# A three-layer EdgeConv plus relational graph network on one core: rows that no edge owns are skipped by the gathers instead of fetched

## The chip, the cores and the metric

The kernel runs on one core of a Trainium2 chip. The metric is the device time of one execution in microseconds (us). The core has five engines that matter here: TensorE (PE in the profile, PEld for its weight loads), VectorE (DVE), ScalarE (ACT), GpSimd (POOL) and SyncE (SP, which issues most DMAs). An indirect DMA, which fetches one table row for each of up to 128 partitions by a list of row numbers, is issued by POOL.

## The reference, cut to what matters

There are 12,500 nodes with 128 features and 212,500 directed edges sorted by destination. Three layers of edge convolution are followed by one relational layer:

```python
def _edge_conv(x, src, dst, W1, b1, W2, b2, n_nodes):     # three times, relu between
    xi = x[dst]
    xj = x[src]
    m = jnp.concatenate([xi, xj - xi], axis=-1)
    h = jax.nn.relu(m @ W1 + b1) @ W2 + b2
    agg = jax.ops.segment_max(h, dst, num_segments=n_nodes)
    return jnp.where(jnp.isfinite(agg), agg, 0.0)
...
x = _layernorm(x + edge_conv_stack(x))
# relational layer: row = src + n * rel, inv = 1 / count of row
msg = x[dst] * inv[row][:, None]
agg = segment_sum(msg, row).reshape(r, n, e)
x = _layernorm(x + relu(einsum('rij,rnj->ni', weights, agg)))
```

## The kernel before

**Tiles of edges.** `m @ W1` is split into a part that depends on the destination node (a table in SBUF, `table`) and a part that depends on the source node (a table in device memory, `tab_b`, 12,544 rows of 128 floats). Edges are cut into tiles of 128, and a tile holds edges of one super block of 256 destination nodes only. Each of the 49 super blocks begins a new tile, so the last tile of a super block is filled up with positions whose edges belong to the next super block. There are `NT` = 1,712 tiles of 128 positions, 219,136 positions for 212,500 edges, so 6,636 positions are owned by no edge (3.03%). From the inputs, the super blocks need 1,684 tiles, with 3,052 unowned positions in them, and the 28 last tiles (3,584 positions) are unowned altogether. The fourth gather stage (below) cuts the same number of edges, sorted by source, into `NT2` = 1,708 tiles, with 6,124 unowned positions (2.80%).

**What an unowned position does before the change.** In the first three stages it keeps the source number of the edge that stands there (or a number from the padding), and its row is fetched and computed. Its place in the block, `loc_f`, is `OUT_OF_BLOCK` (256), so the one-hot matrices ignore it. In the fourth stage its row number is its position in the tile (0 to 127), from `iota`.

**A layer's loop.** Tiles are taken in groups of `GT` = 4. For each group POOL issues four indirect DMAs (`gather_body`, L857), each fetching 128 rows of `tab_b` (128 floats each) into one of `HG` = 4 buffers `rows`. POOL waits with `s_p1` until PE has used the buffer four groups ago, and every four groups for the list of row numbers (`s_idx`, copied by ACT, L1323). PE transposes the gathered rows into PSUM (L977), adds the destination part by one-hot products (L979), multiplies by `W2` (L986), and transposes back after the maximum scan (L1001). ACT evicts (L1341, L1353) and copies the block's table rows (L1332). DVE makes the one-hot matrices (L1637, L1639) and does the scan (L1666). SP stores the scanned rows and loads the block numbers. 428 groups make a layer, 1,712 gathers. Between layers POOL fetches the last row of each node (`gather_ends`, L840, 98 indirect DMAs, three times in all).

**The relational stage.** With z = x times each relation's weights stored as `z_tab` (100,352 rows), POOL fetches four tiles per group again (`gather_products`, L918, 427 groups, 1,708 gathers, buffers `got`). PE multiplies each by a one-hot matrix (L1225), which ACT makes (L1416, L1425), and DVE adds the product to the accumulator (L2146).

**Where the row numbers are made.** `edge_stage` (DVE, seven times, each with two sets of 128 tiles) reads windows of destinations and sources, in four parts; PE turns `src_f` and DVE copies it to `idx_all`. `window_work` (DVE, seven times) does the same for the relational stage, with `row2`, and `any2` for the unowned positions. `key_windows` (L865) is one indirect DMA with only 50 partitions (`NST` = 50), and L823 is another; both fetch 512 bytes for each partition.

The order on each engine is the order in which the program is written. Semaphores alone connect the engines.

Of the kernel before, what the change touches and what calls it, by code (L numbers as in the profile page):

```python
# [25 lines left out]
I32 = mybir.dt.int32  # L26
# [6 lines left out]
P = 128  # L33
EPS = 1e-5
BIG = 3.3895313892515355e38
OUT_OF_BLOCK = 256
GT = 4
HG = 4
# [7 lines left out]
def gnn_kernel(nc, x, src, dst, etype, params, w_rel, out):  # L46
    N, C = x.shape
    E = dst.shape[0]
    R = w_rel.shape[0]
    assert C == P  # L50
    NB = -(-N // P)
# [27 lines left out]
    OUT2 = 2 * W2P - 1  # L79
# [22 lines left out]
    with ExitStack() as ctx:  # L102
# [3 lines left out]
        def sem(name):  # L106
            return ctx.enter_context(nc.semaphore(name))
# [7 lines left out]
        iota = sb("iota", [P, P])  # L115
# [35 lines left out]
        a = Area(agg, NBT * P)  # L151
# [29 lines left out]
        a = Area(work, WORK)  # L181
# [14 lines left out]
        a = Area(agg, NBT * P)  # L196
        idx = [a.cut(HT, I32) for _ in range(2)]
# [4 lines left out]
        rows = [a.cut(GT * P).rearrange("p (t f) -> p t f", f=P) for _ in range(HG)]  # L202
# [12 lines left out]
        a = Area(tab_a, TAB)  # L215
# [7 lines left out]
        src_f = [a.cut(P) for _ in range(2)]  # L223
        loc_f = [a.cut(P) for _ in range(2)]
        starts = [a.cut(P) for _ in range(2)]
        stops = [a.cut(P) for _ in range(2)]

        a = Area(work, WORK)
# [95 lines left out]
        def meta_of(k, f, t):  # L325
            at = (k % LG * 4 + f) * GT + t
            return meta[k // LG][:, at:at + 1]
# [42 lines left out]
        s_rows = [sem(f"s_rows{k}") for k in range(HG)]  # L370
        s_st = [sem(f"s_st{k}") for k in range(2)]
        s_sent = sem("s_sent")
        s_found = sem("s_found")
        s_ecol = sem("s_ecol")
        s_base = sem("s_base")
# [431 lines left out]
        def _(pool):  # L807
# [35 lines left out]
            for l in range(3):  # L843
                if l > 0:
                    for c in range(NC):
                        gather_ends(l, c, c % 2)
                for s in range(2):
                    pool.wait_ge(s_bd[s], 8 * NC * (l + 1))
                def gather_body(i, many=LG):
                    for k in range(many):  # L850
                        at = Lt(l, i, k)
                        if at.j == 0:
                            pool.wait_ge(s_idx[at.h], at.n + 1)
                        pool.wait_ge(s_p1, at.G + 1)
                        tick()
                        for t in range(GT):
                            g.indirect_dma_start(rows[at.j][:, t, :], None, tab_b,  # L857
                                                 bass.IndirectOffsetOnAxis(
                                                     ap=idx[at.h][:, at.j * GT + t:at.j * GT + t + 1], axis=0)
                                                 ).then_inc(s_rows[at.j], 16)  # L860

                def key_windows():
                    pool.wait_ge(s_rk, RK_WIN)
                    tick()
                    g.indirect_dma_start(win2_i, None, key_s.rearrange("(a n) -> a n", a=1),  # L865
                                         bass.IndirectOffsetOnAxis(ap=at2, axis=1)).then_inc(s_kwin, 16)

                def pair_windows(n):
                    pool.wait_ge(s_pairs, 16)
                    pool.wait_ge(s_from2, n + 1)  # L870
                    tick()
                    for s in range(2):
                        g.indirect_dma_start(win2[s].rearrange("p e f -> p (e f)"), None,
                                             pairs.rearrange("n f -> (n f)").rearrange("(a n) -> a n", a=1),
                                             bass.IndirectOffsetOnAxis(ap=from2[s], axis=1)).then_inc(s_win2[s], 16)

                if l < 2:
                    with loop(pool, 0, NL) as i:
                        gather_body(i)
                else:  # L880
                    with loop(pool, 0, 9) as i:
                        gather_body(i)
                    key_windows()
                    with loop(pool, 9, WIN_BODY) as i:
                        gather_body(i)
                    for n in range(NQ // 2):
                        pair_windows(n)
                        with loop(pool, WIN_BODY + 2 * n, WIN_BODY + 2 * n + 2) as i:
                            gather_body(i)
                    with loop(pool, WIN_BODY + NQ, NL) as i:  # L890
                        gather_body(i)
                gather_body(NL, many=OV)
                if l == 0:
                    pool.wait_ge(s_af, NC + 1)
                    g.iota(row_base, [[GT * P, NTP // GT], [1, GT]], base=1 - GT, channel_multiplier=0, **exact
                           ).then_inc(s_base, 1)
                if l == 1:
                    pool.wait_ge(s_keys, 16)
                if l == 2:
                    for s in range(2):  # L900
                        pool.wait_ge(s_crs[s], 16 * (NQ // 2))
                for s in range(2):
                    pool.wait_ge(s_st[s], 16 * (NG // 2) * (l + 1))
                pool.wait_ge(s_sent, 16 * (l + 1))
                if l == 0:
                    pool.wait_ge(s_er, 6)
# [4 lines left out]
            def gather_products(i, many):  # L911
                for k in range(many):
                    if k % LG == 0:
                        pool.wait_ge(s_cr[k // LG], 16 * (i + 1))
                    pool.wait_ge(s_pr, i * LR + k + 1)
                    tick()
                    for t in range(GT):
                        g.indirect_dma_start(got[k % HG][:, t, :], None, z_tab,  # L918
                                             bass.IndirectOffsetOnAxis(ap=meta_of(k, 0, t).bitcast(I32), axis=0)
                                             ).then_inc(s_got[k % HG], 16)  # L920

            with loop(pool, 0, NL2) as i:
# [545 lines left out]
        def _(dve):  # L1468
# [87 lines left out]
            def edge_stage(n, part):  # L1556

                if part == 0:
                    dve.wait_ge(s_win[min(n, 1)], 64 if n == 0 else 32 * (NQ - 2))
                    for s in range(2):  # L1560
                        v.tensor_copy(win_base[s], base_f[:, 2 * n + s:2 * n + s + 1])
                        v.tensor_copy(dst_f[s], dst_w[2 * n + s])
                        last = v.tensor_copy(src_f[s], src_w[2 * n + s])
                    last.then_inc(s_wv, 1)
                elif part == 1:
                    dve.wait_ge(s_wv, n * WV + 1)
                    for s in range(2):
                        v.tensor_scalar(loc_f[s], dst_f[s][:, 1:P + 1], win_base[s], float(OUT_OF_BLOCK), ALU.subtract, ALU.min)
                        v.tensor_tensor(starts[s], dst_f[s][:, 1:P + 1], dst_f[s][:, 0:P], ALU.not_equal)
                        last = v.tensor_tensor(stops[s], dst_f[s][:, 1:P + 1], dst_f[s][:, 2:P + 2], ALU.not_equal)  # L1570
                    last.then_inc(s_wv, 1)
                elif part == 2:
                    dve.wait_ge(s_wv, n * WV + 2)
                    for s in range(2):
                        v.tensor_scalar(starts[s], starts[s], -2.0, 1.0, ALU.mult, ALU.add)
                        last = v.tensor_scalar(stops[s], stops[s], -float(OUT_OF_BLOCK), float(OUT_OF_BLOCK), ALU.mult, ALU.add)
                    last.then_inc(s_wv, 1)
                else:
                    dve.wait_ge(s_wv, n * WV + 3)
                    for s in range(2):  # L1580
                        after(dve, s_store[s], 48 * n)
                    for s in range(2):
                        v.tensor_scalar(cut_b[s], starts[s], BIG, None, ALU.mult)
                        v.tensor_copy(loc_b[s], loc_f[s])
                        last = v.tensor_tensor(stops[s], stops[s], loc_f[s], ALU.max)
                    last.then_inc(s_wv, 1)

# [337 lines left out]
            def window_work(n, part):  # L1925
# [23 lines left out]
                elif part == 5:  # L1949
                    dve.wait_ge(s_wv2, 4 * n + 2)  # L1950
                    for s in range(2):
                        v.scalar_tensor_tensor(out=row2[s], in0=loc2[s], scalar=float(OUT2), in1=row2[s],
                                               op0=ALU.is_lt, op1=ALU.mult)
                        last = v.scalar_tensor_tensor(out=any2[s], in0=loc2[s], scalar=float(OUT2), in1=iota[:, :],
                                                      op0=ALU.is_ge, op1=ALU.mult)
                    last.then_inc(s_wv2, 1)
                elif part == 6:
                    dve.wait_ge(s_wv2, 4 * n + 3)
# [252 lines left out]
```

## Time and profile before

| | |
|---|---|
| median of 3 runs | 9462.51 us (9452.86 to 9466.43) |
| profiled execution, its own time | 9459.5 us |
| its span, first to last instruction | 9457.6 us |
| POOL busy | 6941.5 us (73%) |
| PE busy | 6691.3 us (71%) |
| DVE, ACT busy | 56%, 52% |
| mean granted TensorE clock | 0.91 |

The page gives busy time of each engine, groups of instructions by source line with the idle time ahead of them and what ended it, and the timeline gives single instructions. Idle time marked "issue" is time in which the engine waited for nothing that the profile shows. Register and semaphore instructions are not counted as busy.

### The profile page before, as it was taken

What the parts mean: (1) busy time and instruction counts of PE and PEld (TensorE: products, weight loads), DVE (VectorE), ACT (ScalarE), POOL (GpSimd) and SP (SyncE); (2) the same over time, 40 slices, a digit from 0 to 9 for tenths busy, and PEclk for the clock granted to TensorE, in tenths of its full rate; (3) what the DMA queues carried; (4) which work ended last, traced back from release to release, by engine and by line L of the source; (5) the groups of instructions that cost most, each with busy time, mean ns of one, the idle gap of its engine ahead of it and who ended that gap; (6) DMA issues with size and microseconds to landing.
All of it is one profiled execution on the core that took longest, in us unless ns stands there. A gap on an engine that the chain in (4) does not pass through costs nothing.

```text
span 9457.6 us, 159685 instructions
## 1 busy us (share of the span) xinstructions
PE 6691.3 (71%) x41098; PEld 5236.2 (55%) x41098; DVE 5269.7 (56%) x9597; ACT 4895.9 (52%) x11866; POOL 6941.5 (73%) x7196
## 2 busy tenths in 40 slices
PE   6777777876677777777667777777768555555555
PEld 6666666665555666666555665666644333333333
DVE  4666667665577666667546555555556333333334
ACT  3444444443344444444434444444446777777776
POOL 5777777776777777777777777777764777777775
PEclk9999999998899999989989999999999777777777
DMA  6665666664455555565545666656656222222222
GB/s 161 159 160 158 159 158 160 156 161 120 134 153 148 151 152 151 148 148 147 148 127 152 165 160 163 162 156 159 157 158 240 54 54 54 54 54 54 54 54 67
DMA packets 896218, 1260.59 MB, mean 133 GB/s; under 512 B 185847, under 2 KB 601079, under 8 KB 895270
## 3 DMA queue, kind: packets, MB, share of 16 engines
q1 hardware_dynamic: 650494, 784.23, 27.5%
q0 software_dynamic: 230048, 471.99, 22.9%
q8 instruction: 158, 2.59, 0.1%
q10 hardware_dynamic: 15408, 0.88, 0.1%
q14 instruction: 110, 0.90, 0.0%
HBM read 834.14 MB, written 424.01 MB: 133 GB/s over the span
## 4 chain that ended last, share of the span: by engine, by line
POOL 17%; issue 12%; PE 11%; DMA 7%; DVE 2%; ACT 1%; POOLq 0%; DVEq 0%; ACTq 0%; SPq 0%
POOL agg L857 10%; PE ps L1225 6%; POOL work L918 6%; DMA work<-z_tab,work 4%; DMA agg<-tab_b,agg 3%; PE ps L979 2%; POOL work L840 1%; DVE tab_a L2146 1%; PE ps L1201 1%; PE ps L1202 1%; PE ps L977 1%; ACT agg L1274 0%; PE ps L986 0%; ACT tab_a L1425 0%; DVE work L2168 0%
## 5 line engine op out<-in xcount | busy, mean ns | idle before, releaser
L857 POOL DMA_INDIRECT agg<-tab_b,agg x5136 | 4991.5, 972 | 1625.4 <-issue 1533.1
L979 PE MATMUL ps<-tab_a 128*128 128x128 f32 x20544 | 3076.1, 284 | 1.9 <-issue 1.9
L979 PEld LDWEIGHTS ps<-tab_a 128*128 128x128 f32 x20544 | 2872.3, 202 | 2.4 <-issue 2.4
L977 PE MATMUL ps<-ident,agg 128*128 128x128 f32 x5136 | 1480.4, 288 | 1600.8 <-DMA agg<-tab_b,agg 1517.3
L1666 DVE TENSOR_TENSOR_SCAN agg<-agg,ps 128x512 f32<-128x512 bf16 x1284 | 1639.5, 1277 | 1693.6 <-PE ps L986 1691.3
L1341 ACT ACTIVATE agg<-ps 128x512 f32<-128x512 f32 x1284 | 766.5, 597 | 3483.6 <-PE ps L979 3459.4
L918 POOL DMA_INDIRECT work<-z_tab,work x1708 | 1611.8, 944 | 576.2 <-issue 454.4
L1225 PE MATMUL ps<-tab_a,work 128*128 128x256 f32 x3416 | 1224.3, 521 | 917.9 <-DMA work<-z_tab,work 634.4
L977 PEld LDWEIGHTS ps<-ident,agg 128*128 128x128 f32 x5136 | 752.7, 147 | 1836.7 <-issue 1409.3
L1332 ACT ACTIVATE tab_a<-tab_a 128x256 f32 x5136 | 1714.1, 404 | 59.0 <-issue 48.2
L1225 PEld LDWEIGHTS ps<-tab_a,work 128*128 128x128 f32 x3416 | 839.4, 257 | 1303.2 <-DVE tab_a L2146 1110.6
L2146 DVE TENSOR_TENSOR tab_a<-ps,tab_a 128x256 f32 x1708 | 724.3, 424 | 1417.2 <-PE ps L1225 1246.2
L986 PE MATMUL ps<-agg,w 128*128 128x512 f32 x2568 | 1342.5, 605 | 0.0
L1425 ACT ACTIVATE tab_a<-tab_a,work 128x256 f32<-128x256 f32 x1708 | 883.7, 588 | 469.0 <-issue 469.0
L1637 DVE SCALAR_TENSOR_TENSOR tab_a<-agg,pidx,ps 128x512 f32<-128x512 bf16 x1284 | 933.1, 727 | 45.6 <-ACT agg L1341 44.1
L1639 DVE SCALAR_TENSOR_TENSOR tab_a<-agg,pidx_up,ps 128x512 f32<-128x512 bf16 x1284 | 950.1, 740 | 0.0
L1001 PEld LDWEIGHTS ps<-ident,agg 128*128 128x128 f32 x5136 | 610.0, 141 | 469.1 <-issue 464.3
L1001 PE MATMUL ps<-ident,agg 128*128 128x128 f32 x5136 | 787.3, 276 | 4.7 <-DVE agg L1666 2.3
L1416 ACT ACTIVATE tab_a<-work 128x256 f32<-128x256 f32 x1708 | 727.4, 496 | 59.7 <-DMA work<-col_rel 5.1
L1353 ACT ACTIVATE agg<-ps 128x512 f32<-128x512 f32 x1284 | 738.3, 575 | 17.6 <-PE ps L1001 14.5
L1658 DVE TENSOR_SCALAR agg<-iota_b,agg 128x128 bf16<-128x128 bf16 x1712 | 331.4, 275 | 457.8 <-PE ps L993 440.8
L840 POOL DMA_INDIRECT work<-scan_rows,endrow x294 | 288.7, 982 | 194.3 <-issue 99.6
(252 smaller groups left out, 2963.3 us busy)
## 6 DMA issues: line engine op xcount, KB each, us to landing
agg<-row_two SPq DMA_DIRECT2D x1284, 256.0 KB
scan_rows<-agg SPq DMA_DIRECT2D x1284, 256.0 KB
agg<-tab_b,agg POOLq DMA_INDIRECT x5136
z_tab<-tab_a SPq DMA_DIRECT2D x84, 512.0 KB, 3.7
work<-z_tab,work POOLq DMA_INDIRECT x1708
tab_b<-work SPq DMA_DIRECT2D x42, 448.0 KB, 3.1
work<-in_x SPq DMA_DIRECT2D x26, 448.0 KB, 5.3
z_tab<-work SPq DMA_DIRECT2D x14, 512.0 KB, 3.8
```

Source lines behind the costliest of these rows:

```text
L857: g.indirect_dma_start(rows[at.j][:, t, :], None, tab_b, bass.IndirectOffsetOnAxis(ap=idx[at.h][:, at.j * GT + t:at.j * GT + t + 1], axis= ...
L918: g.indirect_dma_start(got[k % HG][:, t, :], None, z_tab, bass.IndirectOffsetOnAxis(ap=meta_of(k, 0, t).bitcast(I32), axis=0)).then_inc(s_ ...
L977: mm(to, rows[at.j][:, t, :], ident[:, :], is_transpose=True, start=True, stop=False)
L979: last = mm(to, tabs[at.s][:, t, h * P:(h + 1) * P], hot_t[at.s][:, h, t * P:(t + 1) * P], start=False, stop=(h == 1))
L986: mm(ps[:, 2 + at.s, :], w2[:, l], h1[at.s], start=True, stop=True).then_inc(s_p2, 1)
L1001: last = tr(ps[:, 4 + at.s, t * P:(t + 1) * P], scan[at.s][:, t * P:(t + 1) * P], ident[:, :])
L1225: last = mm(flat[:, to:to + W2P], got[k % HG][:, t, :], hot_r[k % 4][:, t, :], start=True, stop=True)
L1332: last = a_(tabs[s][:, t, :], table[:, bass.ds(blk[t] * W2P, W2P)], ACT.Copy)
L1425: last = a_(hot_r[k % 4][:, t, :], off_r[k % 2][:, t, :], ACT.Relu, scale=meta_of(k, 3, t), bias=meta_of(k, 2, t))
L1637: v.scalar_tensor_tensor(out=hot_t[at.s][:, 0, :], in0=locs[at.k], scalar=pidx[:, 0:1], in1=ps[:, at.s, :], op0=ALU.is_equal, op1=ALU.bypass)
L1639: v.scalar_tensor_tensor(out=hot_t[at.s][:, 1, :], in0=locs[at.k], scalar=pidx_up[:, 0:1], in1=ps[:, at.s, :], op0=ALU.is_equal, op1=ALU.b ...
L1666: v.tensor_tensor_scan(scan[at.s], cuts[at.k], ps[:, 2 + at.s, :], scan[1 - at.s][:, GT * P - 1:GT * P], ALU.min, ALU.max).then_inc(s_scan, 1)
```

## The change

Four things are edited. (1) In `edge_stage` the source number of an unowned position becomes `NB * P` = 12,544, one beyond the last row of `tab_b`: a new tile `off_f` is made by one tensor_scalar for each set and merged by one maximum. (2) In `window_work` an unowned position gets row number `NB * P * R` = 100,352, one beyond `z_tab`, in place of its position in the tile. (3) All gathers of `gather_body` and `gather_products` get a highest allowed number (`bounds_check`) and `oob_is_err=False`, by which a number beyond it makes no transfer and no error. The bound is handed to the instruction in a register, and the built program sets that register ahead of each of these gathers. The other indirect DMAs are as before. (4) Since a skipped row keeps what its buffer held, POOL clears the four buffers `rows` (128 x 512 floats each) once ahead of the first layer's gathers, and waits for it.

```diff
+        off_f = [a.cut(P) for _ in range(2)]
...
+        s_clean = sem("s_clean")
...
                 for s in range(2):
                     pool.wait_ge(s_bd[s], 8 * NC * (l + 1))
+                if l == 0:
+                    for k in range(HG):
+                        g.memset(rows[k], 0.0).then_inc(s_clean, 1)
+                    pool.wait_ge(s_clean, HG)
...
                             g.indirect_dma_start(rows[at.j][:, t, :], None, tab_b,
                                                  bass.IndirectOffsetOnAxis(
-                                                     ap=idx[at.h][:, at.j * GT + t:at.j * GT + t + 1], axis=0)
+                                                     ap=idx[at.h][:, at.j * GT + t:at.j * GT + t + 1], axis=0),
+                                                 bounds_check=NB * P - 1, oob_is_err=False
                                                  ).then_inc(s_rows[at.j], 16)
...
                         g.indirect_dma_start(got[k % HG][:, t, :], None, z_tab,
-                                             bass.IndirectOffsetOnAxis(ap=meta_of(k, 0, t).bitcast(I32), axis=0)
+                                             bass.IndirectOffsetOnAxis(ap=meta_of(k, 0, t).bitcast(I32), axis=0),
+                                             bounds_check=NB * P * R - 1, oob_is_err=False
                                              ).then_inc(s_got[k % HG], 16)
...
                         v.tensor_scalar(starts[s], starts[s], -2.0, 1.0, ALU.mult, ALU.add)
+                        v.tensor_scalar(off_f[s], loc_f[s], float(OUT_OF_BLOCK), float(NB * P), ALU.is_ge, ALU.mult)
...
                         v.tensor_copy(loc_b[s], loc_f[s])
+                        v.tensor_tensor(src_f[s], src_f[s], off_f[s], ALU.max)
...
-                        last = v.scalar_tensor_tensor(out=any2[s], in0=loc2[s], scalar=float(OUT2), in1=iota[:, :],
-                                                      op0=ALU.is_ge, op1=ALU.mult)
+                        last = v.tensor_scalar(any2[s], loc2[s], float(OUT2), float(NB * P * R), ALU.is_ge, ALU.mult)
```

Apart from the register, nothing else moves on any engine. On POOL, ahead of the first layer's loop, the program before has the last of the 28 window loads and then the jump into the loop (`tab_b` is the source table, `agg` the memory in which the buffers `rows` lie):

```order
L830 DMA work<-src_pad,tab_a 128x128
L878 UNCONDITIONAL_BRANCH
L878 BRANCH_PREFETCH_HINT
L878 ISA
L854 ISA
L857 DMA agg<-tab_b,agg 128x128 x4
```

In the changed program the same place reads:

```order
L832 DMA work<-src_pad,tab_a 128x128
L853 MEMSET agg 128x512 x4
L885 UNCONDITIONAL_BRANCH
L885 BRANCH_PREFETCH_HINT
L885 ISA
L860 ISA
L863 DMA agg<-tab_b,agg 128x128 x4
```

The four memsets stand ahead of the first gather, and the gathers themselves keep their number and order.

## Rows read from the trace of the kernel before

**Rows 1.** The page's part 1, busy us (share of span) xinstructions:

```profile
PE 6691.3 (71%) x41098; PEld 5236.2 (55%) x41098; DVE 5269.7 (56%) x9597; ACT 4895.9 (52%) x11866; POOL 6941.5 (73%) x7196
```

**Rows 2.** Groups of POOL: out<-in xcount | busy, mean ns | idle before:

```profile
L857 POOL DMA_INDIRECT agg<-tab_b,agg x5136 | 4991.5, 972 | 1625.4 <-issue 1533.1 <-PE ps L979 75.6 <-ACT agg L1323 16.5
L918 POOL DMA_INDIRECT work<-z_tab,work x1708 | 1611.8, 944 | 576.2 <-issue 454.4 <-PE ps L1225 65.8 <-DMA work<-col_rel 56.0
```

**Rows 3.** Timeline of POOL, first layer: start us, us, instruction, idle before:

```profile
1513.87 0.94 POOL L857 DMA_INDIRECT agg<-tab_b,agg  x1 [0.30 <-issue]
1515.12 0.94 POOL L857 DMA_INDIRECT agg<-tab_b,agg  x1 [0.30 <-issue]
1516.37 0.94 POOL L857 DMA_INDIRECT agg<-tab_b,agg  x1 [0.30 <-issue]
1517.61 0.94 POOL L857 DMA_INDIRECT agg<-tab_b,agg  x1 [0.30 <-ACT agg L1323]
...
1521.39 0.94 POOL L857 DMA_INDIRECT agg<-tab_b,agg  x1 [0.30 <-PE ps L979]
```

**Rows 4.** Each gather line by itself: duration ns min/median/max, first and last start:

```profile
L857 POOL DMA_INDIRECT agg<-tab_b,agg x5136: 938/944/4941, 108.8 to 7017.3; - x198
L918 POOL DMA_INDIRECT work<-z_tab,work x1708: 940/944/962, 7260.2 to 9391.3; - x190
```

**Rows 5.** Busy time by stretch: first layer, third layer, relational stage:

```profile
core 0: us, PE busy (x) PEld busy (x) DVE busy (x) ACT busy (x) POOL busy (x), PEclk, DMA share, GB/s
108.70:2248.00 2139.30, 1683.47 (x12790) 1358.23 (x12790) 1468.32 (x3675) 1013.81 (x2660) 1618.31 (x1710) 0.97 0.61 158
4841.00:7018.30 2177.30, 1642.67 (x11217) 1335.79 (x11218) 1187.53 (x1551) 1015.91 (x2660) 1650.24 (x1724) 0.97 0.61 158
7260.00:9393.00 2133.00, 1222.32 (x3408) 837.96 (x3408) 721.46 (x1702) 1594.50 (x3415) 1611.80 (x1708) 0.77 0.21 54
```

**Rows 6.** Groups of PE that wait for gathered rows:

```profile
L977 PE MATMUL ps<-ident,agg 128*128 128x128 f32 x5136 | 1480.4, 288 | 1600.8 <-DMA agg<-tab_b,agg 1517.3
L1225 PE MATMUL ps<-tab_a,work 128*128 128x256 f32 x3416 | 1224.3, 521 | 917.9 <-DMA work<-z_tab,work 634.4
```

**Rows 7.** POOL instructions with one call or other shapes, same columns as Rows 2:

```profile
L865 POOL DMA_INDIRECT work<-key_s,work x1 | 1.0, 957 | 0.3 <-issue 0.3
L823 POOL DMA_INDIRECT agg<-dst_pad,agg x1 | 1.1, 1106 | 15.6 <-DVE agg L1505 15.6
L810 POOL MEMSET agg<- 1x620 int32 x1 | 0.6, 604 | 0.3 <-POOLq L2199 0.3
```

**Rows 8.** Timeline ahead of the first gather, ACT and POOL:

```profile
102.73 0.21 ACT L1323 ACTIVATE agg<-idx_all 128x16 int32<-128x16 int32 x1 [0.25 <-issue]
108.77 0.94 POOL L857 DMA_INDIRECT agg<-tab_b,agg  x1 [27.14 <-issue]
```

**Rows 9.** DVE groups with the shapes of the added and replaced operations:

```profile
L1576 DVE TENSOR_SCALAR tab_a<-tab_a 128x128 f32<-128x128 f32 x14 | 3.4, 243 | 0.0
L1585 DVE TENSOR_TENSOR tab_a<-tab_a 128x128 f32<-128x128 f32 x14 | 4.0, 283 | 0.7 <-issue 0.7
L1954 DVE SCALAR_TENSOR_TENSOR work<-work,iota 128x128 f32<-128x128 f32 x14 | 4.0, 287 | 0.0
```

**Rows 10.** Timeline of POOL, second layer: gathers that took longer:

```profile
4399.81 3.09 POOL L857 DMA_INDIRECT agg<-tab_b,agg  x1 [0.31 <-issue]
4403.21 0.94 POOL L857 DMA_INDIRECT agg<-tab_b,agg  x1 [0.30 <-issue]
```

**Rows 11.** The page's part 3, queue: packets, MB, share of 16 engines:

```profile
q1 hardware_dynamic: 650494, 784.23, 27.5%
q0 software_dynamic: 230048, 471.99, 22.9%
```

## The prediction

> **What bounds the kernel now.** I read the busy shares first. No engine is full over the whole span: POOL has 73%, PE 71% [rows 1]. Such a share is an average over stages and hides what POOL's idle time is, so I went to the groups of POOL. The 5,136 gathers of the three layers and the 1,708 of the relational stage have 972 and 944 ns of busy time each, and almost all of the idle time before them is "issue", not a wait for anybody [rows 2]. The timeline shows the form of it: a gather of 0.94 us, 0.30 us of nothing, the next gather, without end, so one starts every 1.25 us [rows 3]. The reader should see that the gap is the same 0.30 us where the row names PE or ACT as the releaser. These are the group changes, at which POOL has a semaphore wait and a register operation of its own to do. So the released wait had long been satisfied, and the small sequencer work between two gathers costs nothing visible.
>
> Then the stretches: 1,712 gathers at 1.249 us are 2138 us, and the first layer's stretch is 2139 us. 1,708 at 1.249 are 2133 us, and the relational stage is 2133 us; the third layer's 2177 us hold some longer gathers [rows 5]. In these stretches POOL is the bound from the first gather to the last. In one group's 5.0 us PE works 1683/428 = 3.9 us in the layers (2.9 us in the relational stage, where ACT has 1594/427 = 3.7 us), and PE's largest wait is for the gathered rows [rows 5, 6]. The DMA engines are at 0.61 and 0.21 of their time, so transfers aren't what holds the queue up [rows 5]. The time of this kernel is therefore 6,844 times what POOL spends on one gather, plus stages that the change doesn't touch: each nanosecond on each gather is 6.84 us of the total, 0.07%. Everything below turns on what POOL pays for one gather with the bound and the skipping.
>
> **What the change removes.** It removes transfers: 3 x 6,636 + 6,124 = 26,032 rows of 512 bytes, 13.3 MB of the 472 MB that POOL's queue moves [rows 11]. I cost this at nothing, because what PE waits for is the gather that POOL hasn't issued yet, and not a long transfer. The cover is POOL's own pace: as long as gathers start 1.25 us apart and the DMA engines are 0.61 busy, a transfer that is 3% smaller only lands a little earlier in a wait that POOL ends. Nor does POOL issue fewer instructions: all 6,844 gathers stay, those of the 28 wholly unowned tiles too.
>
> Does a gather with fewer rows cost POOL less? The gathers of the relational stage lie between 940 and 962 ns over 1,708 of them [rows 4]. The one warm indirect DMA with 50 partitions in place of 128 (same 512 bytes each) took 957 ns, against 944; another with 50, the very first of the program, took 1106 [rows 7]. So 78 rows less bring nothing, and the 3.8 rows less in a mean gather should bring nothing either. For the other side, were the whole 944 ns proportional to rows, 3.03% would be 29 ns on each of 5,136 gathers and 2.80% 26 ns on 1,708: 147 + 45 = 192 us saved. That is the lower bound.
>
> **What the change adds to a gather.** First, a register set ahead of each. POOL's register operations at group changes lie inside the same 0.30 us gap [rows 3], so I take nothing; if it were exposed, it would lengthen the gap in each row. Second, the comparison of 128 numbers with the bound and the leaving out of rows on both sides, reads and writes. No row of the trace has such a gather. Its lower end is nothing, if the comparison fits beside work that takes 944 ns anyhow. For its upper end I take the nearest elementary work of POOL, one element after another in one partition: the memset of 620 elements took 604 ns, 0.97 ns each [rows 7], so 128 elements are 125 ns, or 6,844 x 0.125 = 855 us. Between the two I choose by the row that stands nearest, the warm 50-row gather: work per row is so small a part of a gather that 78 rows moved it by 13 ns at the most. I take 13 ns as the size of something small and real that is done for each gather, 6,844 x 0.013 = 89 us. That it is above zero is a judgement: instructions have to be executed for the check on the engine that has no slack, and 2.4 ns a gather are enough to be seen.
>
> The Trainium skill has a rule that speaks against the change more strongly. 
>
> **What it adds elsewhere.** The four memsets have 512 elements in each partition. At 0.97 ns these are 0.5 us each, 2.0 us, and about 0.3 us for the wait on `s_clean`. Queued behind them on POOL is the first gather, and everything waits for POOL from there on. The row numbers are ready at 102.9 us, and the first gather starts at 108.8 us, with nothing to wait for that is shown [rows 8], so POOL has a start-up of its own there that the memsets may partly overlap. I take 2.3 us in full. DVE gets 14 tensor_scalar of 243 ns and 14 maxima of 283 ns, 7.4 us in seven portions, and in the third layer 14 operations become 44 ns cheaper [rows 9]. DVE has 1468 us of work in a first layer of 2139 us [rows 5], and the six portions inside the layer end long before their row numbers are used. The first portion, 1.05 us, lies ahead of the last of the table stores that open the layer. Cost nothing; without that cover 1 us.
>
> **The sum.** Profiled time 9459.5 + 2.3 + 89 = 9551 us. The median of the runs is 3 us above this execution, so I say 9553 us, 1.0% slower.
>
> **The rivals.**
>
> A. *The check is free.* It hides beside the fixed part of a gather. For it: the constancy of 944 ns in all gathers whatever their data, and the hidden register work. Against it: POOL has no other work to hide it behind. Result 9462.5 + 2.3 = 9465 us. It holds while the extra is under (19 - 2.3)/6.84 = 2.4 ns.
>
> B. *A gather's cost falls with its rows.* This is the case on the other side. Place: the 0.94 us in each gather. Price: up to 192 us, so 9273 us; it decides as soon as a skipped row saves more than the check costs. For it: nothing but that rows must be written by somebody; against it the 50-row gather. A part of it, 20 to 60 us, is as likely as the whole.
>
> C. *The check works through the rows one by one with a decision on each.* Then a gather grows by more than the 125 ns of the upper end, and the kernel goes above 10,320 us. For example, if the 944 ns are 7.4 ns for each of 128 rows and a decision adds half of that, a gather grows by 472 ns and the kernel to 9462 + 3230 = 12,690 us; PE, ACT and DVE would only wait longer. Against it: 128 rows and 50 cost the same, so work seems not to go row by row. The skill's rule above would be this case.
>
> D. *Contention.* Single gathers of the second layer took 3.09 us [rows 10] beside DVE's sorting, which is why the mean of the layers is 972. If the new gather touches SBUF more, these grow. The whole excess before is 5,136 x 28 ns = 144 us, and doubling it gives +144 us: inside my case.
>
> **How the numbers follow.** A measurement of this kernel can tell about 0.2%, 19 us. My case, something small from 2.4 to 125 ns a gather: 0.42 (9482 to 10,320 us). A: 0.32. B: 0.18, of which 0.10 below 9400 us. C: 0.08. The range leaves out C and the far part of B, 0.18 in all, and so goes from 9400 to 10,320 us. My case alone, at 5 to 60 ns, would be 9500 to 9875 us. Faster 0.18, same 0.32, slower 0.42 + 0.08 = 0.50.
>
> **What would show it.** The profile after should have the gathers of both lines as before in number, with a median above 944 ns by 5 to 60 ns in the relational stage, where nothing disturbs them, or a gap longer than 0.30 us if the register work is exposed. The gathers of the 28 unowned tiles, the last ones of each layer, are the test of B: if they are shorter than the others, rows do cost. Packets of POOL's queue should fall by about 26,000. PE's wait for gathered rows should grow by what the gathers grow. I am wrong if the median stays at 944 (then A), if it falls, or if the added time sits at the start of the first layer instead of in every gather.

## The result

The changed kernel takes 9839.35 us (median of 4 runs, 9832.66 to 9853.8) against 9464.28 us (4 runs, 9452.86 to 9466.43). The ratio is 1.0402, with a 95% interval from 1.0389 to 1.0415. The direction was forecast; the size was not: 375 us instead of 91, or 4.0% instead of 1.0%.

The page of the changed kernel, in the form of [rows 1] (busy us, share of the span, instructions) and, for POOL's queue, of [rows 11] (packets, MB, share of the 16 engines):

```profile
PE 6833.1 (69%) x41098; PEld 5364.7 (54%) x41098; DVE 5276.5 (54%) x9625; ACT 4901.0 (50%) x11866; POOL 7331.0 (74%) x7200
...
q0 software_dynamic: 230048, 460.27, 20.9%
```

POOL has 389.5 us more to do with four instructions more. The groups of POOL (count, busy, mean ns of one, idle before) say where, and answer to [rows 2]:

```profile
L863 POOL DMA_INDIRECT agg<-tab_b,agg x5136 | 5286.3, 1029 | 1608.6 <-issue 1507.3 <-PE ps L987 98.0 <-ACT agg L1331 3.4
L925 POOL DMA_INDIRECT work<-z_tab,work x1708 | 1705.2, 998 | 576.1 <-issue 479.6 <-DMA work<-col_rel 56.0 <-PE ps L1233 40.5
...
L853 POOL MEMSET agg<- 128x512 f32 x4 | 1.9, 532 | 19.2 <-DMA tab_b<-work 19.2
```

The layers' gathers grew by 294.8 us and the relational stage's by 93.4 us, together 388.2 of the 394.3 us by which this execution (9853.8 us) is longer than the one profiled before (9459.5 us). The idle time between them didn't grow. Each line by itself (min/median/max ns, first and last start) shows that the gathers are longer throughout, the shortest too; compare [rows 4]:

```profile
L863 POOLq MOVE  x5136: 29/29/38, 105.2 to 7303.1; - x198
L863 POOL DMA_INDIRECT agg<-tab_b,agg x5136: 992/1000/5169, 112.2 to 7317.6; - x198
```

```profile
L925 POOL DMA_INDIRECT work<-z_tab,work x1708: 992/1000/1015, 7562.6 to 9787.0; - x190
```

The median rose from 944 to 1000 ns. 6,844 x 56 ns are 383 us, 2% above the measured 375. Below, the same form of gather has a median of 997 ns in four kernels, two of which are the changed one with a single edit, so 3 of the 56 ns belong to this execution or its chip. The MOVE that sets the bound's register takes 29 ns. The timeline of POOL in the first layer (start, us, instruction, idle before) shows the same 0.30 us gap as in [rows 3], so the MOVE lies inside it:

```profile
1513.91 1.00 POOL L863 DMA_INDIRECT agg<-tab_b,agg  x1 [0.30 <-issue]
1515.21 1.00 POOL L863 DMA_INDIRECT agg<-tab_b,agg  x1 [0.30 <-PE ps L987]
1516.52 1.00 POOL L863 DMA_INDIRECT agg<-tab_b,agg  x1 [0.30 <-issue]
```

What waits on POOL pays: PE's wait for the layers' rows rose from 1517.3 [rows 6] to 1687.0 us, and in the relational stage from 634.4 to 769.0 us.

### The profile page after: what moved, and what is told of

Its sections match the earlier page's. It is cut to its first block, busy times and chain, and to the rows that moved or that the text cites. A ratio compares the mean times of both kernels' runs of the same rounds, so it can differ in the third digit from the quotient of the medians.

```text
span 9851.9 us, 166561 instructions
## 1 busy us (share of the span) xinstructions
PE 6833.1 (69%) x41098; PEld 5364.7 (54%) x41098; DVE 5276.5 (54%) x9625; ACT 4901.0 (50%) x11866; POOL 7331.0 (74%) x7200
## 3 DMA queue, kind: packets, MB, share of 16 engines
q0 software_dynamic: 230048, 460.27, 20.9%
## 4 chain that ended last, share of the span: by engine, by line
issue 18%; POOL 15%; PE 9%; DMA 6%; DVE 1%; POOLq 1%; ACT 1%; ACTq 0%; DVEq 0%; SPq 0%
POOL agg L863 7%; POOL work L925 7%; PE ps L1233 4%; DMA agg<-tab_b,agg 3%; DMA work<-z_tab,work 3%; PE ps L987 2%; POOL work L842 1%; PE ps L985 1%; PE ps L1209 1%; PE ps L1210 1%; PE ps L994 0%; ACT agg L1282 0%; POOLq L925 0%; POOLq L863 0%; DVE work L2177 0%
## 5 line engine op out<-in xcount | busy, mean ns | idle before, releaser
L863 POOL DMA_INDIRECT agg<-tab_b,agg x5136 | 5286.3, 1029 | 1608.6 <-issue 1507.3
L987 PE MATMUL ps<-tab_a 128*128 128x128 f32 x20544 | 3163.8, 289 | 5.9 <-issue 5.9
L987 PEld LDWEIGHTS ps<-tab_a 128*128 128x128 f32 x20544 | 2949.7, 207 | 6.6 <-issue 6.6
L985 PE MATMUL ps<-ident,agg 128*128 128x128 f32 x5136 | 1503.7, 293 | 1789.7 <-DMA agg<-tab_b,agg 1687.0
L925 POOL DMA_INDIRECT work<-z_tab,work x1708 | 1705.2, 998 | 576.1 <-issue 479.6
L1233 PE MATMUL ps<-tab_a,work 128*128 128x256 f32 x3416 | 1254.6, 531 | 980.7 <-DMA work<-z_tab,work 769.0
L1233 PEld LDWEIGHTS ps<-tab_a,work 128*128 128x128 f32 x3416 | 864.3, 265 | 1371.5 <-DVE tab_a L2155 1166.4
```

The source lines that it names most:

```text
L863: g.indirect_dma_start(rows[at.j][:, t, :], None, tab_b, bass.IndirectOffsetOnAxis(ap=idx[at.h][:, at.j * GT + t:at.j * GT + t + 1], axis= ...
L925: g.indirect_dma_start(got[k % HG][:, t, :], None, z_tab, bass.IndirectOffsetOnAxis(ap=meta_of(k, 0, t).bitcast(I32), axis=0), bounds_chec ...
L985: mm(to, rows[at.j][:, t, :], ident[:, :], is_transpose=True, start=True, stop=False)
L987: last = mm(to, tabs[at.s][:, t, h * P:(h + 1) * P], hot_t[at.s][:, h, t * P:(t + 1) * P], start=False, stop=(h == 1))
L1233: last = mm(flat[:, to:to + W2P], got[k % HG][:, t, :], hot_r[k % 4][:, t, :], start=True, stop=True)
```

## The experiments

The first eight ran in two sets of four, the last four in a third, each set on one chip beside the kernel before. Ratios are against the kernel before of the same set.

### The bound alone, nothing to skip

```diff
                                                      ap=idx[at.h][:, at.j * GT + t:at.j * GT + t + 1], axis=0),
+                                                 bounds_check=NB * P - 1, oob_is_err=False
...                                        (kernel before; the same in gather_products)
```

> The kernel before with the bound and oob_is_err=False on all 6,844 gathers of the four stages; every row number stays valid, nothing is skipped, no memset, no edits on VectorE. Theory 1 (the bounded form of the gather costs about 56 ns whatever it skips): median gather 1000 ns in both stages, time 9464 + 6,844 x 0.055 = 9840 us, ratio 1.040. Rival 2 (the cost comes from rows that are skipped): median 944 ns, ratio 1.000.

9836.63 us, ratio 1.0388 (1.037 to 1.0406), 373 us more than the kernel before. The gathers of the relational stage, all numbers valid:

```profile
L919 POOL DMA_INDIRECT work<-z_tab,work x1708: 992/997/1009, 7548.4 to 9768.1; - x190
```

997 ns without one skipped row. The bounded form of the instruction carries the whole loss within the noise, 373 of 375 us, and rival 2 falls.

### The edits without the bound

```diff
-  float(NB * P), ALU.is_ge          (off_f, changed kernel)
+  float(NB * P - 1), ALU.is_ge
-  float(NB * P * R), ALU.is_ge      (any2)
+  float(NB * P * R - 1), ALU.is_ge
-  bounds_check=..., oob_is_err=False
```

> The changed kernel with its VectorE edits, its four memsets and its wait, but without a bound: unowned positions get the number of the last valid row in place of one beyond the table, so all rows are fetched as before. Theory 1: gathers at 944 ns, time before plus 2 to 4 us for the memsets (ratio 1.0002 to 1.0004). Rival 3 (a good part of the loss sits in the edits around the gathers, such as VectorE's work or the late first gather): more than 20 us above before.

9543.48 us, ratio 1.0079 (1.0065 to 1.0093): 80 us more, and theory 1 was wrong about this kernel. The median gather stayed at 944 ns (the layers' mean was 975 instead of 972, 15 us in all):

```profile
L863 POOL DMA_INDIRECT agg<-tab_b,agg x5136: 938/944/5112, 108.7 to 7069.4; - x198
L924 POOL DMA_INDIRECT work<-z_tab,work x1708: 940/944/961, 7332.8 to 9463.7; - x190
```

So the time is lost elsewhere. The last 20 us of gathers of the first and of the third layer (columns as in [rows 5]), where only unowned tiles are gathered, all from one row of the table:

```profile
2236.00:2256.00 20.00, 13.04 (x90) 10.70 (x90) 10.85 (x24) 6.92 (x19) 15.52 (x16) 0.91 0.94 97
7049.00:7069.00 20.00, 13.01 (x80) 10.81 (x79) 7.84 (x9) 6.91 (x18) 15.12 (x17) 0.90 0.99 72
```

The same stretches in the kernel before. There the windows of these tiles are cut off at the end of the edge list and fall on its padding, which counts up from 0, so each of these gathers reads the 128 different rows 0 to 127:

```profile
2230.00:2250.00 20.00, 14.76 (x118) 11.85 (x117) 13.64 (x33) 9.33 (x25) 15.12 (x17) 1.00 0.54 158
6997.00:7017.00 20.00, 15.74 (x114) 12.80 (x113) 10.31 (x12) 9.20 (x24) 15.12 (x17) 1.00 0.43 128
```

And 20 us of the unowned tiles of the first layer in the changed kernel, where these gathers fetch nothing:

```profile
2323.00:2343.00 20.00, 14.93 (x108) 12.62 (x109) 11.88 (x29) 7.61 (x20) 15.21 (x16) 0.92 0.39 107
```

POOL issues at about one pace in all; with the shared row the DMA engines are at 0.94 and 0.99 instead of 0.54 and 0.43 and move less (97 and 72 GB/s against 158 and 128). After the last gather of a stage the work waits for rows on their way, as the chain of work that ended last shows for the kernel without the bound (start, us, what; first and third layer, relational stage):

```profile
2253.67 19.17 DMA agg<-tab_b,agg
7069.38 19.64 DMA agg<-tab_b,agg
9463.67 14.42 DMA work<-z_tab,work
```

That left two readings, the row that thousands of positions share or the edits on VectorE and the memsets. The experiment with the same numbers as before, below, separates them.

### The bound in the relational stage alone

```diff
                                              bass.IndirectOffsetOnAxis(ap=meta_of(k, 0, t).bitcast(I32), axis=0),
+                                             bounds_check=NB * P * R - 1, oob_is_err=False
```

> The kernel before with the bound in the relational stage alone (1,708 gathers), all numbers valid. Theory 1: these gathers at 1000 ns and the layers' at 944, time 9464 + 1,708 x 0.055 = 9558 us, ratio 1.010: the cost is additive by gathers. Rival 2: ratio 1.000. Rival 4 (other engines absorb part of a slower POOL in this stage, since ACT has 3.7 us in a group of 5.0): below 1.006.

9547.76 us, ratio 1.0091 (1.0076 to 1.0107), 84 us. The layers' gathers stayed at 944 ns, these took 997; 1,708 x 53 ns are 91 us. The stretch of these gathers (same columns):

```profile
7259.00:9480.00 2221.00, 1241.59 (x3408) 856.02 (x3408) 720.78 (x1701) 1593.81 (x3414) 1700.71 (x1708) 0.77 0.20 52
```

It became 88 us longer than the 2133 us of [rows 5]. The cost adds up by gathers, and no other engine absorbs it: rival 4 falls with rival 2.

### One register for all gathers

```diff
+            top_b = g.to_reg(NB * P - 1)
+            top_z = g.to_reg(NB * P * R - 1)
...
-                                                 bounds_check=NB * P - 1, oob_is_err=False
+                                                 bounds_check=top_b, oob_is_err=False
```

> The changed kernel with its two bounds set in registers once, ahead of everything, in place of a 29 ns MOVE ahead of each gather. Theory 1 (the comparison itself costs it): no change against the changed kernel, 9840 us, gathers at 1000 ns, gap 0.30 us. Rival 5 (the MOVE is part of the 56 ns): gathers or gaps shorter by up to 29 ns, 9640 us.

9841.9 us, ratio 1.0396 (1.038 to 1.0412), with gathers at 997 ns. The MOVE costs no time here, as the unchanged gap said, and rival 5 falls.

### A relational stage that skips everything

```diff
-  any2[s], loc2[s], float(OUT2), float(NB * P * R), ALU.is_ge, ALU.mult
+  any2[s], loc2[s], -1e6, float(NB * P * R), ALU.is_ge, ALU.mult
```

> The changed kernel with every position of the relational stage sent beyond the table: its 1,708 gathers fetch nothing at all, so the relational sums are left out of the result. Theory 1 (a gather's cost on POOL doesn't depend on how many rows it transfers): these gathers stay at 1000 ns and the kernel at 9840 us. Rival 6 (skipping rows saves a little, and 3% of rows were too few to show it): if 128 skipped rows save even 10% of 944 ns, 906 ns and 160 us less. If skipping costs: above 1000 ns.

The comparison with -1e6 is true for every position, so every row number of the stage lies beyond the table, and the relational sums are missing from the result. 9833.84 us, ratio 1.0395 (1.0377 to 1.0412). These gathers, and the page's line of POOL's queue:

```profile
L925 POOL DMA_INDIRECT work<-z_tab,work x1708: 992/997/1013, 7547.0 to 9766.5; - x190
```

```profile
q0 software_dynamic: 230048, 350.82, 17.1%
```

The queue carried 121 MB less than before, and a gather that fetches nothing costs POOL the same 997 ns as one that fetches 128 rows. A skipped row is worth nothing on POOL, at 3% or at 100%; rival 6 falls. The number of packets is still 230,048.

### Fewer partitions, with and without the bound

```diff
-  g.indirect_dma_start(got[k % HG][:, t, :], None, z_tab,
+  g.indirect_dma_start(got[k % HG][0:64, t, :], None, z_tab,       (or 0:16)
-  bass.IndirectOffsetOnAxis(ap=meta_of(k, 0, t).bitcast(I32), axis=0)
+  bass.IndirectOffsetOnAxis(ap=meta_of(k, 0, t)[0:64].bitcast(I32), axis=0)
```

> The kernel before with the gathers of the relational stage over 64 partitions in place of 128; the other half of each tile's rows is left out of the sums. No bound. My reading before was that rows cost POOL nothing: 944 ns, or 957 as the 50-row gather. Rival (work per row, as 7.4 ns for each of 128): 472 ns.

> As the 64-partition gathers without bound, with the bound in the relational stage alone (half of the rows left out again). If the bound's cost is per row, 28 ns above the plain 64-row gather; if it is per instruction, 56 ns above it.

> Gathers of 16 partitions with the bound in the relational stage (7 of 8 rows left out of the sums). Cost per row: 7 ns above a plain gather; per instruction: 56 ns above it. If rows themselves cost nothing, about 1000 ns.

> Gathers of 16 partitions without bound in the relational stage (7 of 8 rows left out of the sums). If a plain gather costs 0.55 ns per row as between 128 and 64 rows, 909 - 48 x 0.55 = 883 ns, and the bound's cost at 16 rows is 7 ns. If the bound had a fixed part of 23 ns and 0.23 ns per row, plain would be 890 - 27 = 863 ns.

Each gather names only the first 64 or 16 rows of its tile, and the other rows are missing from the sums; the bounded ones have the bound of the relational stage besides. The gathers' times are medians over 1,708 of them in one profiled execution; each of these four kernels ran once. The lines, in this order: 64 plain, 64 bounded, 16 bounded, 16 plain.

```profile
L918 POOL DMA_INDIRECT work<-z_tab,work x1708: 904/909/925, 7256.9 to 9327.7; - x190
```

```profile
L918 POOL DMA_INDIRECT work<-z_tab,work x1708: 942/947/963, 7267.5 to 9403.2; - x190
```

```profile
L918 POOL DMA_INDIRECT work<-z_tab,work x1708: 886/890/922, 7258.2 to 9296.7; - x190
```

```profile
L918 POOL DMA_INDIRECT work<-z_tab,work x1708: 842/847/867, 7252.0 to 9217.8; - x190
```

| rows in a gather | plain, ns | bounded, ns | bound costs, ns | kernel plain, us | kernel bounded, us |
|---|---|---|---|---|---|
| 128 | 944 | 997 | 53 | 9463.81 | 9547.76 |
| 64 | 909 | 947 | 38 | 9395.90 | 9471.38 |
| 16 | 847 | 890 | 43 | 9285.71 | 9365.35 |

The whole kernels differ by 84, 75 and 80 us, the last pair on two chips.

Two things follow. Rows do cost POOL something when they are named in the instruction: 35 ns from 64 to 128, 62 ns from 16 to 64. So my reading of the 50-row gather [rows 7] was wrong. And the bound's price depends little on the rows: 43, 38 and 53 ns for 16, 64 and 128; why 64 rows have the smallest isn't shown. My forecasts for this series missed: the plain 64-row gather took 909 ns, not 944 or 957; the bound cost neither 28 and 7 ns (per row) nor a constant 56; and the 16-row plain gather took 847, not 883 or 863. Most of the price is paid once for an instruction; if the price of 16 rows were all per row, 128 rows would cost 344 ns.

### Same numbers as before, with the edits

```diff
-  float(NB * P), ALU.is_ge          (off_f, changed kernel, no bound)
+  0.0, ALU.is_ge
+  (any2 as in the kernel before, from iota)
```

> The changed kernel without the bound, with its added VectorE operations (the added number is 0.0 in place of 12,544, so the maximum changes nothing), its memsets and its wait, and with the row numbers of the kernel before in all unowned positions. Theory 7 (the 79 us of the edits without a bound came from thousands of reads of one and the same row at the end of each stage, not from the edits): 9464 + 2 us, ratio 1.000 to 1.001. Rival 3 (VectorE's work or the memsets cost it): 9543 us again.

9472.64 us, ratio 1.0001 (0.9992 to 1.001). With the same memsets, the same wait and the same added operations on VectorE, the 80 us are gone. They belonged to the row that the unowned positions shared. Whether any row would do, or only the last one of the table, isn't shown.

### A number beyond the bound as an error

```diff
-  bounds_check=NB * P - 1, oob_is_err=False      (the bound alone, as above)
+  bounds_check=NB * P - 1
```

> The kernel before with the bound on all 6,844 gathers, but with a number beyond it an error in place of being passed over; all numbers are valid. If the price is that of comparing: 997 ns and 9837 us again. If it is that of being ready to leave rows out silently: 944 ns and 9464 us.

9938.61 us, ratio 1.0496 (1.048 to 1.0512).

```profile
L919 POOL DMA_INDIRECT work<-z_tab,work x1708: 1006/1011/1028, 7622.1 to 9866.4; - x190
```

1011 ns, 67 above a plain gather, 14 above the silent form, and neither of the two forecasts (997 or 944). Being silent isn't what costs; the form that reports costs more, though no number lies beyond the bound.

### Leaving out instructions instead of rows

```diff
-    NT2 = -(-((E + NS * (P - 1)) // P) // GT) * GT
+    NT2 = 1684
...
+            dve.wait_ge(s_cr[1], 16 * (NL2 + 1))
             sums(0, 0)
```

> The kernel before, no bound, with 1,684 tiles in the relational stage in place of 1,708: the 24 wholly unowned tiles aren't gathered at all. The result is complete for this input only; other inputs could need up to 1,708 tiles. Theory 1 (POOL pays per gather instruction): 24 x 1.249 = 30 us less, ratio 0.9968. Rival (the end of the stage isn't paced by POOL): ratio 1.000.

9431.98 us, ratio 0.9962 (0.9949 to 0.9976), 36 us less than the kernel before, in 5 runs from 9429.92 to 9440.67.

```profile
L918 POOL DMA_INDIRECT work<-z_tab,work x1684: 940/945/962, 7262.2 to 9363.9; - x188
```

24 gathers fewer at 945 ns each, unchanged. The added wait covers the last load of row numbers, which no gather waits for any more. Of the versions that give the whole result, this is the only one that beats both kernels. It does so for inputs that fit into 1,684 tiles, as these do, and not for every sorted list of this length.

## Why the prediction was wrong

**What bounds the kernel: right.** The time goes by POOL's time for a gather. The bound in one stage alone (84 us against 91 from the median gather), in all (373 against 363) and the fewer tiles (-36 against -30) follow it within 11 us each.

**Transfers removed: right that they are worth nothing.** POOL's queue moved 11.7 MB less than the 472 MB of before (I had 13.3 MB; the 1.6 MB between them I can't explain). The packets, however, didn't fall by 26,000, and this sign failed: their number is 230,048 in both, and over all queues there are 2,606 more of under 512 B. A packet isn't a row. The 24 gathers left out took 768 packets with them, 32 for each gather of 128 rows, and gathers of 64 or 16 rows, or with all rows skipped, left the number at 230,048.

**Rows against POOL's time: right for skipped rows, by a wrong argument.** I took one warm gather with 50 partitions at 957 ns as evidence that rows cost nothing. The 16- and 64-row gathers show that rows cost 0.5 to 1.3 ns each; why the 50-row one isn't cheaper is open. It was one instruction of another line with other operands, and I built a bound on it. Rival B is nonetheless false for skipped rows: 128 of them saved 0 ns. The sign named for B says the same. The last gathers of the changed kernel's relational stage belong to wholly unowned tiles, and they take as long as all others; this is the last one (timeline of POOL):

```profile
9787.03 1.00 POOL L925 DMA_INDIRECT work<-z_tab,work  x1 [0.30 <-issue]
```

**The step that failed is the size of the added term.** "I take 13 ns as the size of something small and real": it is 53 to 56 ns, four times as much. The 13 ns were the spread of that one comparison by rows, and they would have bounded a cost per row only. The bound's price is mostly paid once for an instruction, and no number of rows could have bounded it. The upper end of 125 ns per gather held, but by distance: it was a price per element, and that isn't how the cost arises. The measured time lies inside the range of 9400 to 10,320 us, in the case with 0.42, and the 56 ns and 9839 us also lie inside the narrower 5 to 60 ns and 9500 to 9875 us given for that case. It is a factor in a term, not the mechanism.

**The register: right.** Setting it ahead of each gather costs 29 ns that lie in the gap; taking it out changed nothing.

**The memsets and VectorE: right within what can be told.** The memsets took 1.9 us (2.0 expected), and DVE had 6.8 us more to do, as worked out (7.4 less 0.6). With them, the first gather started 3.4 us later in the changed kernel (112.2 us against 108.8), and the kernel with all edits but no bound is at 1.0001.

**Rival A** (the check is free) fell with the bound-only kernel. **Rival C** (a decision for each row, one after another) fell too: its price was to be above 125 ns, and it would have grown with the rows.
**PE's wait: right in sign only.** It was to grow by what the gathers grow. In the layers it grew by 170 us for 295 us of gathers, in the relational stage by 135 for 93. Over all stages PE was also busy 142 us longer with the same instructions, at a mean granted clock of 0.90 instead of 0.91, so its wait doesn't measure the gathers' growth.

What in the instruction takes these 38 to 56 ns isn't shown by any run.

## What to carry to other kernels

Where a queue of indirect gathers issued by GpSimd sets the pace, count instructions first: here a row that is passed over costs as much as one that is fetched, a gather that names 16 rows in place of 128 saves only 10% (847 against 944 ns), and the bound costs 5.6% of each gather. If padding must be fetched, let it read rows that differ; if a whole instruction is padding, don't issue it. And a price that is unknown for an instruction isn't bounded by how its time depends on the rows: a cost can be paid once.

## What the runs showed of the hardware that I had not expected

Many reads of one row were slow. With all unowned positions naming the same row of 512 bytes, the last tiles of a layer kept the DMA engines 0.94 to 0.99 busy at 72 to 97 GB/s, where the same gathers of differing rows needed 0.54 and 0.43 at 158 and 128 GB/s. It cost 80 us in a kernel whose median gather was not one nanosecond longer. The kernel before had been spared this because each of these gathers named 128 different rows; that all 28 gathers named the same 128 did no such harm.

A gather of 128 rows whose violations of the bound are errors takes 1011 ns, one whose violations are silent 997, and one without a bound 944. And 128 rows that are passed over cost POOL the same 997 ns as 128 that are fetched.
